# An FFT layer's way back to positions: products into seven PSUM banks, layernorm factors two groups at a time, and the first unit's sum moved forward

## What is computed

```python
    y = jnp.fft.irfft(Xf * Kf.T[None, :, :], n=n, axis=1)[:, :length, :]
    z = y + x * D[None, None, :]
    r = x + z
    ...
    out = (r - mu) * jax.lax.rsqrt(var + LN_EPS) * ln_w + ln_b
    ...
x = x + _L0_attn_ref(xn, ...) + _L0_ffn_ref(xn, ...)
xn = _layernorm(x, axis=-1)
x = x + _L1_attn_ref(xn, ...) + _L1_ffn_ref(xn, ...)
```

## Time and profile before

| what | us |
|---|---|
| median of 3 runs | 912.46 (911.31 to 914.74) |
| the profiled execution's own time | 913.24 |
| its span | 911.1 |
| TensorE busy | 800.2 (88%) |
| VectorE busy | 642.5 (71%) |
| ScalarE busy | 573.1 (63%) |
| chain that ended last: TensorE's share | 56% |

### The profile page before, as it was taken

One profiled execution on the slowest core, in us unless ns is written; L12 is line 12 of the kernel. 1 busy time (PEld: TensorE's weight loads), 2 busy tenths in 40 slices (PEclk: granted clock), 3 DMA queues, 4 the chain that ended last, 5 costly groups with the idle time before them and its releaser, 6 DMA issues.

```text
span 911.1 us, 11973 instructions
## 1 busy us (share of the span) xinstructions
PE 800.2 (88%) x4082; PEld 620.1 (68%) x4082; DVE 642.5 (71%) x1472; ACT 573.1 (63%) x1022; POOL 184.3 (20%) x246
## 2 busy tenths in 40 slices
PE   6964317569999999699999999999999998999998
PEld 6522207446666664377788788878888887899997
DVE  6699205278885485696997889777777775877875
ACT  5840102125555554698987998799898986665564
POOL 0077770006776574000100000000000000000000
PEclk9976555779999999799999999999999999999999
DMA  8534325217777653132441121112121210000000
GB/s 265 204 133 140 122 76 159 66 43 230 230 244 217 195 184 104 23 85 55 102 81 39 37 58 47 40 42 49 47 46 47 47 47 0 8 18 12 19 18 24
DMA packets 79466, 82.16 MB, mean 90 GB/s; under 512 B 11248, under 2 KB 63728, under 8 KB 79152
## 3 DMA queue, kind: packets, MB, share of 16 engines
q1 hardware_dynamic: 68688, 67.98, 26.1%
q0 software_dynamic: 6496, 12.92, 5.5%
q10 hardware_dynamic: 4224, 0.52, 0.4%
HBM read 57.69 MB, written 23.70 MB: 89 GB/s over the span
## 4 chain that ended last, share of the span: by engine, by line
PE 56%; ACT 3%; DVE 3%; POOL 1%; issue 1%; DVEq 0%; ACTq 0%; POOLq 0%
PE ps L1769 17%; PE ps L1771 16%; PE ps L1770 16%; PE ps L2090 3%; PE ps L1954 3%; POOL y_rows L675 1%; ACT hid L914 0%; DVE hid_lo L1683 0%; PE ps L2116 0%; ACT L914 0%; ACT L892 0%; ACT hid_hi L915 0%; PE ps L1935 0%; ACT xn L885 0%; DVE stats L1410 0%
## 5 line engine op out<-in xcount | busy, mean ns | idle before, releaser
L1683 DVE TENSOR_TENSOR hid_lo<-hid,hid_hi 128x512 fp32r<-128x512 f32 x256 | 176.4, 690 | 76.9 <-ACT hid_hi L915 69.5
L914 ACT ACTIVATE hid<-ps,b_sb 128x512 f32<-128x512 f32 x256 | 177.7, 694 | 44.4 <-PE ps L1771 17.5
L915 ACT ACTIVATE hid_hi<-ps,b_sb 128x512 fp32r<-128x512 f32 x256 | 175.6, 686 | 0.0
L1769 PE MATMUL ps<-xt_hi,w_lo 128*128 128x512 f32 x256 | 104.3, 408 | 0.0
L1769 PE MATMUL ps<-hid_hi,w_lo 128*128 128x512 f32 x256 | 101.4, 396 | 1.9 <-DVE hid_lo L1683 1.8
L1771 PE MATMUL ps<-xt_hi,w_hi 128*128 128x512 f32 x256 | 102.1, 399 | 0.0
L1770 PE MATMUL ps<-hid_lo,w_hi 128*128 128x512 f32 x256 | 101.6, 397 | 0.0
L1770 PE MATMUL ps<-xt_lo,w_hi 128*128 128x512 f32 x256 | 100.9, 394 | 0.0
L1771 PE MATMUL ps<-hid_hi,w_hi 128*128 128x512 f32 x256 | 100.6, 393 | 0.0
L675 POOL DMA_INDIRECT y_rows<-yo,row_of x76 | 80.9, 1064 | 71.3 <-issue 66.9
L633 POOL DMA_INDIRECT x_slots<-xn,slot x64 | 68.1, 1063 | 63.3 <-DVE expert_of L1190 44.2
(11 more groups left out here) (332 smaller groups left out, 1720.2 us busy)
## 6 DMA issues: line engine op xcount, KB each, us to landing
gate_row<-gates_dram SPq DMA_DIRECT2D x64, 256.0 KB, 4.9
wc<-w_split SPq DMA_DIRECT2D x19, 682.0 KB
x_slots<-prod SPq DMA_DIRECT2D x11, 520.0 KB, 10.9
w_split<-wc SPq DMA_DIRECT2D x8, 682.0 KB
xc<-x_slots SPq DMA_DIRECT2D x19, 260.0 KB
wst<-w SPq DMA_DIRECT2D x16, 256.0 KB
wd<-w SPq DMA_DIRECT2D x19, 192.0 KB
acc<-y_rows POOLq DMA_DIRECT2D x14, 256.0 KB, 4.9
```

What stands on the lines that cost most here:

```text
L914: nc.scalar.activation(hid1[:, u % 4], ps[:, u % 4], ACT.Gelu_apprx_tanh, bias=b1_sb[:, u:u + 1])
L915: nc.scalar.activation(hid1_hi[:, u % 4], ps[:, u % 4], ACT.Gelu_apprx_tanh, bias=b1_sb[:, u:u + 1]).then_inc(hid1_done, 1)
L1683: tt(hid1_lo[:, u % 4], hid1[:, u % 4], hid1_hi[:, u % 4].bitcast(F32), sub).then_inc(hid1_lo_done, 1)
L1769: mm(dst, a_lo, b_hi, start=first, stop=False)
```

## The change

The products of the eight groups go into seven banks (0, 1, 2, 3, 4, 5, 7, and 3 again for group 7) instead of four. Banks 4 and 5 belong to the chunk loop until its last output is copied, so group 4 waits for `y_copied`. Group 7 waits for groups 0 to 3 to be normalised, and `turn1(0)` stands before group 7 instead of after it. The wait for all eight groups moves from before up1(0, 0) to before up1(0, 3), the first unit that writes bank 3 again. Factors are made for two groups at a time: four roots and four passes of `norm_factors` over 8 columns instead of eight over 4; they now live in `mid1` and `mid1_mv`. `first_sum` moves on VectorE from after group 5's factors to after the second pair's, ahead of residual(4); its root and normalisation on ScalarE come before the third pair's root. The copy of `xt1_hi` on ScalarE moves ahead of the third pair's normalisations, `gate_exp(0)` ahead of the fourth pair's; on VectorE `low1(0)` moves between residual(6) and residual(7), and `gate_logits(0)` and `gate_shift(0)` ahead of the fourth pair's factors.

```diff
-AHEAD = 5
+POSITION_BANK = (0, 1, 2, 3, 4, 5, 7, 3)
...
-            def root(i, g, signal, stats_ready):
-                act_e.wait_ge(stats_ready, g + 1)
-                if g >= 2:
-                    act_e.wait_ge(norm1_done, g - 1)
-                nc.scalar.activation(mid[:, g % 2, i, 0], mid_mv[:, g % 2, i, :, 1], ACT.Sqrt, bias=eps[:]).then_inc(signal, 1)
-            def normalised(dst, src, i, g, ready, signal):
-                act_e.wait_ge(ready, g + 1)
+            def root(first, end, signal, stats_ready, n):
+                t = slice(first * B, end * B)
+                act_e.wait_ge(stats_ready, n)
+                nc.scalar.activation(mid1[:, 0, t], mid1_mv[:, t, 1], ACT.Sqrt, bias=eps[:]).then_inc(signal, 1)
+            def normalised(dst, src, g, ready, n, signal):
+                act_e.wait_ge(ready, n)
                 for b in range(B):
-                    last = nc.scalar.activation(dst[:, b], src[:, b], ACT.Identity, bias=mid[:, g % 2, i, 2, b:b + 1],
-                                                scale=mid[:, g % 2, i, 0, b:b + 1])
+                    t = slice(g * B + b, g * B + b + 1)
+                    last = nc.scalar.activation(dst[:, b], src[:, b], ACT.Identity, bias=mid1[:, 2, t], scale=mid1[:, 0, t])
                 last.then_inc(signal, 1)
+            def pair_normalised(i):
+                for g in (2 * i, 2 * i + 1):
+                    normalised(rows3(g), for_batch(ps[:, POSITION_BANK[g]]), g, norm1_ready, i + 1, norm1_done)
...
-            root(0, 0, root1_done, mid_stats)
-            for i in range(G):
-                if i == 1:
+            for i in range(G // 2):
+                if i == 2:
+                    act_e.wait_ge(norm1_done, 1)
+                    root(0, 1, root2_done, mid_stats2, 1)
+                    normalised(for_batch(xn1[:, 0]), rows3(0), 0, norm2_ready, 1, xn1_done)
+                root(2 * i, 2 * i + 2, root1_done, mid_stats, 2 * i + 2)
+                if i == 0:
                     for n in range(TURNS - 1, len(pieces1)):
                         weights_high(n)
-                if i + 1 < G:
-                    root(0, i + 1, root1_done, mid_stats)
-                normalised(rows3(i), for_batch(ps[:, i % 4]), 0, i, norm1_ready, norm1_done)
-                if i == AHEAD:
-                    root(1, 0, root2_done, mid_stats2)
-                    normalised(for_batch(xn1[:, 0]), rows3(0), 1, 0, norm2_ready, xn1_done)
-            act_e.wait_ge(xt1_done, 1)
-            copy(xt1_hi[:, 0], ps[:, 6]).then_inc(xt1_hi_done, 1)
-            gate_exp(0)
+                if i == 2:
+                    act_e.wait_ge(xt1_done, 1)
+                    copy(xt1_hi[:, 0], ps[:, 6]).then_inc(xt1_hi_done, 1)
+                if i == 3:
+                    gate_exp(0)
+                pair_normalised(i)
...
-            def norm_factors(i, g, root_done_, signal):
-                m, mv_ = mid[:, g % 2, i], mid_mv[:, g % 2, i]
-                dve.wait_ge(root_done_, g + 1)
-                inverse_root(m[:, 0], mv_[:, :, 1], m[:, 1])
-                stt(m[:, 2], mv_[:, :, 0], -1.0, m[:, 0], mul, mul).then_inc(signal, 1)
+            def norm_factors(first, end, root_done_, n, signal):
+                t = slice(first * B, end * B)
+                dve.wait_ge(root_done_, n)
+                inverse_root(mid1[:, 0, t], mid1_mv[:, t, 1], mid1[:, 1, t])
+                stt(mid1[:, 2, t], mid1_mv[:, t, 0], -1.0, mid1[:, 0, t], mul, mul).then_inc(signal, 1)
 
             def residual(g):
                 dve.wait_ge(y_done, g + 1)
-                moments(for_batch(ps[:, g % 4]), 0, g, mid_stats)
+                moments(for_batch(ps[:, POSITION_BANK[g]]), 0, g, g, mid_stats)
+            def pair_factors(i):
+                norm_factors(2 * i, 2 * i + 2, root1_done, i + 1, norm1_ready)
...
-                moments(rows3(0), 1, 0, mid_stats2)
-                norm_factors(1, 0, root2_done, norm2_ready)
+                moments(rows3(0), 1, 0, 0, mid_stats2)
+                norm_factors(0, 1, root2_done, 1, norm2_ready)
...
             residual(0)
-            for i in range(G):
-                if i + 1 < G:
-                    residual(i + 1)
-                norm_factors(0, i, root1_done, norm1_ready)
-                if i == 2:
-                    for n in range(TURNS - 1, len(pieces1)):
-                        weights_low(n)
-                    scale_rows(0)
-                    layer0_sum(0)
-                if i == AHEAD:
-                    first_sum()
+            residual(1)
+            pair_factors(0)
+            for n in range(TURNS - 1, len(pieces1)):
+                weights_low(n)
+            residual(2)
+            scale_rows(0)
+            layer0_sum(0)
+            residual(3)
+            pair_factors(1)
+            first_sum()
+            residual(4)
+            residual(5)
+            pair_factors(2)
+            residual(6)
+            low1(0)
+            residual(7)
             dve.wait_ge(biases_in, 48)
-            low1(0)
             gate_logits(0)
             gate_shift(0)
+            pair_factors(3)
...
-                if g >= 4:
-                    pe.wait_ge(norm1_done, g - 3)
+                if g == 4:
+                    pe.wait_ge(y_copied, final_chunk + 1)
+                if g == G - 1:
+                    pe.wait_ge(norm1_done, 4)
                 for m in range(HM):
                     if g == 0:
                         pe.wait_ge(products_done, PAIR * (m + 1))
                     for part_ in range(2):
-                        last = mm(ps[:, g % 4], inv[:, m, part_, t * P:(t + 1) * P], z[:, m + HM * (t // 2), c, part_],
+                        last = mm(ps[:, POSITION_BANK[g]], inv[:, m, part_, t * P:(t + 1) * P], z[:, m + HM * (t // 2), c, part_],
...
-            for g in range(G):
+            for g in range(G - 1):
                 positions(g)
             turn1(0)
+            positions(G - 1)
             logits1(0)
...
+                if is_at(g, u, 0, 3):
+                    pe.wait_ge(norm1_done, G)
                 three(ps[:, u % 4], w_hi[:, w], w_lo[:, w], xh, xl).then_inc(up1_done, 1)
...
             pe.wait_ge(w1_lo_done, len(pieces1))
-            pe.wait_ge(norm1_done, G)
             for u in range(3):
```

More of the change, by code:

```diff
@@ L125, in program @@
         b2_sb = sb("b2_sb", [P, E])
-        mid = sb("mid", [P, 2, 2, 3, B])
-        mid_mv = sb("mid_mv", [P, 2, 2, B, 2])
         mid1 = sb("mid1", [P, 3, T])
@@ L1402, in _, with moments @@
             all_chunks(dve, chunk_hidden)
-            def moments(src, i, g, signal):
-                if g:
-                    dve.wait_ge(signal, g)
+            def moments(src, i, g, n, signal):
+                if n:
+                    dve.wait_ge(signal, n)
                 for b in range(B):
@@ L1412, in moments @@
                 for b in range(B):
-                    last = nc.vector.bn_aggr(mid_mv[:, g % 2, i, b], stats[:, i * B + b])
+                    last = nc.vector.bn_aggr(mid1_mv[:, g * B + b], stats[:, i * B + b])
                 last.then_inc(signal, 1)
-            def norm_factors(i, g, root_done_, signal):
-                m, mv_ = mid[:, g % 2, i], mid_mv[:, g % 2, i]
-                dve.wait_ge(root_done_, g + 1)
-                inverse_root(m[:, 0], mv_[:, :, 1], m[:, 1])
-                stt(m[:, 2], mv_[:, :, 0], -1.0, m[:, 0], mul, mul).then_inc(signal, 1)
+            def norm_factors(first, end, root_done_, n, signal):
[3 more added lines that the diff above has]
+                stt(mid1[:, 2, t], mid1_mv[:, t, 0], -1.0, mid1[:, 0, t], mul, mul).then_inc(signal, 1)
             def residual(g):
                 dve.wait_ge(y_done, g + 1)
-                moments(for_batch(ps[:, g % 4]), 0, g, mid_stats)
+                moments(for_batch(ps[:, POSITION_BANK[g]]), 0, g, g, mid_stats)
+            def pair_factors(i):
+                norm_factors(2 * i, 2 * i + 2, root1_done, i + 1, norm1_ready)
             def first_sum():
```

## The result

The changed kernel takes 907.93 us (median of 5 runs, 907.15 to 908.93) against 912.46; the ratio is 0.9946 with an interval of 0.9929 to 0.9963. That is 4.5 us less, clear of 1 by the interval and just above the 0.5% that the prediction took as the least that can be told. It lies inside the range and 2.4 above the forecast that goes with the median, 905.5. The profiled execution took 908.93 us with a span of 906.9, 4.3 less than the profiled one of before and 2.7 above the forecast of 906.2. The first rival of the prediction, the falling clock, had put it at 908.8.

The account below looks back on a forecast made before the run. TensorE, busy 88%, was taken to bound the kernel except from 371.9 to the first down1 at 388.99. That start moves to 382.0, 7.0 us less: 913.24 becomes 906.2, or 905.5 against the median; range 904.5 to 910.5.

Parts of the forecast that it names:

- The first rival of the prediction: TensorE's clock falls to half in the tail's new pauses, losing 2.6 us in the expert loop: 908.8 us, chance 0.25.
- The three signs of being wrong: TensorE waits before turn1(0), VectorE stands still at first_sum, or first down1 to the end grows beyond 522.1 us.
- the likeliest case: The first down1 starts 7.0 us earlier with TensorE at full clock: 905.3 to 907.7 us, chance 0.55.
- The place and the mechanism: Only the tail from 371.9 to the first down1 shortens, 17.1 to 10.1 us; everything behind it moves along.
- the layout: VectorE, ScalarE and TensorE laid out anew by measured durations, from residual(1) to a first down1 at about 382.0.
- Banks at nothing: Seven banks gain nothing by themselves, as positions have no pause; they free positions of ScalarE until group 7.
- Pairs: Factors for two groups at once on VectorE: 1.16 us a pass over 8 columns, as over 4; four passes saved, 4.6 us.
- The 0.5 of turn1: Four transposes moved ahead of group 7 on TensorE make it end 0.5 us later, the one cost on the path.
- The rows of first_sum: VectorE's two input rows land 2.9 us after issue, at about 360.4, 0.6 before they are wanted, so no wait.
- The clock: TensorE's two new pauses, each near 3 us and neither as long as 5.0, leave the expert loop at 0.23 us a matmul.
- The drain of a table load: On ScalarE, each load brings a drain, 2.66 us in all; sum 1.4 us smaller, 907.6 us; rival, chance 0.02.
- No time-bound transfer: Rival: a second-stage transfer due at a fixed time holds the end while the experts start earlier; about 912 us, chance 0.05.

Follow-up runs that it names:

- the kernel with four banks: Changed kernel with its products in banks 0 to 3 again and the old waits for normalised groups: 866.64 us, ratio 0.9937 to the kernel before.
- two runs, in both directions: Kernel before with seven banks and group 7's moved wait only: 872.52 us, ratio 0.9994; changed kernel with the old four banks: 866.64 us, ratio 0.9937.
- the run without the rows: Changed kernel whose first_sum adds ln_w twice instead of waiting for its two rows, SyncE waiting for them: 869.56 us in a single execution, no ratio.
- the filled run: Changed kernel with both TensorE pauses filled by unread matmuls, 11 and 9: 866.05 us, ratio 0.9927 to the kernel before.
- the repeated run: Changed kernel measured once more, unaltered, on another chip: 868.12 us, ratio 0.9957 to the kernel before.
- the last one: Changed kernel with group 7 normalised on VectorE, both pauses filled, scale_rows(2) moved into the expert loop: 904.46 us, ratio 0.9906 to the kernel before.
- the old kernel filled: Kernel before with its two pauses around turn1(0) filled by 19 and 16 unread matmuls: 870.87 us, ratio 0.9987.

## Why the prediction was right, and where its size was off

The time lies in the range, but not for the reason that was held likeliest. The three signs of being wrong that the prediction names all came, each in a small measure: VectorE stood still at first_sum for 1.40 us, TensorE was some 0.25 late before turn1(0), and the distance to the end grew by 2.2. The range holds the time because the first rival was priced in it; the likeliest case, 905.3 to 907.7, was missed, and that part of the hit is due to the width of the range.

- **The place and the mechanism** hold: the tail from 371.9 to the first down1, and a unit count behind it. Forecast 382.0, measured 382.55. With the rows in time the layout is right to 0.2: 382.0 - 344.3 = 37.7 forecast from the first start of positions to the first down1, 37.5 in the kernel with four banks.
- **Banks at nothing, the order as the gain**: shown by two runs, in both directions. The text took the banks as cover up to group 6; the run with four banks shows that not even that cover was needed.
- **Pairs**: 1.16 forecast, 1.21 us measured for 8 columns. What pairs are worth by themselves wasn't tried.
- **The 0.5 of turn1** ahead of group 7: measured 369.06 - 368.56 = 0.5. The transposes' own price was right; their late start came on top.
- **The rows of first_sum** were mis-sized. The step took 2.9 us to landing from a median over two transfers, and the second took 4.47; SyncE also issued 0.5 later. So first_sum waited 1.40 instead of nothing. The slack of about 1 us was right. The price is some 0.25 us ahead of turn1(0) and 0.4 in the tail, by the run without the rows.
- **The clock** was the step that failed in the likeliest case. It was held at full with the argument that neither pause was as long as the 5.0 us of before. The fall was priced rightly (2.6 forecast at most, 2.2 read off, 2.1 by the filled run's time and 2.6 by its distance) and given one chance in four; it came in every profile of the changed kernel and of all its forms that had a pause of 2 us or more left. The Trainium skill ("TensorE: Matmul & The Clock Gate", section "What's actually happening") has the state depend on recent activity; this trace agrees, with the clock at half 4.2 us after the last dense work, in spite of three matmuls between. The row with 0.85 at 52 to 53 in the earlier trace rows, a fall 3 us after work had ended, was the better guide than the one of 5.0.
- **The drain of a table load** that the Trainium skill states ("ScalarE: Activation LUTs", section "What ACT_TABLE_LOAD costs") isn't seen: load at 374.39, Exp at 375.68, 1.29 later. The prediction priced it at 1.4 us for the Exp load alone; the Gelu load is on the path too, so by that rule it would have been twice as much.
- **No time-bound transfer** in the second stage: with the clock full, 521.7 us from the first down1 to the end against 522.1 of before.

Together: 7.0 forecast, less some 0.6 for the rows (0.25 ahead of group 7, 0.3 to 0.4 in the tail), is 6.4; less 2.2 for the clock is 4.2, the difference of the spans.

## What to carry to other kernels

When a stage's tail is shortened, look at the pauses that TensorE keeps in it: a shorter wait followed at once by dense work can cost more in clock than a long wait whose slow stretch fell on work that was early. Filling pauses of 2 to 3 us with unread matmuls was worth 2.1 us here beside the 5 of the reordering. And a step that is moved ahead of others must be costed by the latest landing of its inputs, not by the median.

## What the runs showed of the hardware

- A pause of 2.0 to 2.2 us can be enough for half clock: in the repeated run TensorE waited 2.17 us before positions (to 302.65), the window from 302 to 303 has 0.62, and the first 56 matmuls took 25.2 us instead of 24.2. The run without the rows (25.9) and the last one (25.5) show the same there; in the other profiles a pause as long (2.13 to 2.16) left the clock up. With four banks TensorE waited 2.02 us, and the clock fell at about 335.1, 0.3 after work was back.
- The fall can come after work is back (at 341.5 with dense matmuls since 340.5) and behind a stretch of 10-column matmuls with pauses of 0.5 us only ahead of it (at 342.8, in the old kernel filled). Why it fell there these traces don't show.
- The landing of a transfer of 256 KB varies from execution to execution: the second of the two rows took 4.47 us in the changed kernel's first profile, and no more than 3.0 in the kernel with four banks, where first_sum starts at 318.71 without a wait and SyncE issued from 315.32 on. The median of the two is 2.7 to 3.0 us in eight of the fourteen profiles and 3.6 to 3.9 in the six in which first_sum waited; what sets it wasn't found.
